# Two transformer layers on one core: the order of the small tasks between the attention scores, and where the last batches' feed-forward blocks stand

## The reference

```python
x = _layernorm(x + _L0_attn_ref(x, ...))   # 16 heads of 8, full softmax attention
x = _layernorm(x + _L0_ffn_ref(x, ...))    # 128 -> 512, butterfly, exact GELU, butterfly, 512 -> 128
x = _layernorm(x + _L1_attn_ref(x, ...))   # low-rank q and kv, rotary embedding (RoPE), causal attention
x = _layernorm(x + _L1_ffn_ref(x, ...))    # silu(x Wg^T) * (x Wu^T), then Wd^T; 384 hidden, int32 weights / 127
```

## Time and profile before

| | |
|---|---|
| median of 3 runs | 343.15 us (340.76 to 343.46) |
| the profiled execution | 346.31 us, of which the span of the trace is 344.2 us |
| PE busy | 308.4 us, 90% |
| DVE busy | 249.8 us, 73% |
| ACT, POOL busy | 184.2 us (54%), 178.3 us (52%) |
| mean granted clock of TensorE | 0.979 of full speed |

### The profile page before, as it was taken

One profiled execution on the slowest core, in us unless ns is written; L12 is line 12 of the kernel. 1 busy time (PEld: TensorE's weight loads), 2 busy tenths in 40 slices (PEclk: granted clock), 3 DMA queues, 4 the chain that ended last, 5 costly groups with the idle time before them and its releaser, 6 DMA issues.

```text
span 344.2 us, 10412 instructions
## 1 busy us (share of the span) xinstructions
PE 308.4 (90%) x3770; PEld 219.9 (64%) x3770; DVE 249.8 (73%) x941; ACT 184.2 (54%) x396; POOL 178.3 (52%) x299
## 2 busy tenths in 40 slices
PE   8799998899899998999899699899999999976862
PEld 4566665666486566766567457776777777755652
DVE  4897686769587785868839469697989898935454
ACT  3365675465946566565746337465556555545110
POOL 6595372210224252453627939397877747455621
PEclk9999999999999999999989789999999999999989
DMA  6733350011000110203011110111111200001000
GB/s 253 210 136 49 87 130 3 4 31 33 3 3 2 34 33 16 50 4 63 3 33 34 31 28 8 35 33 34 33 34 49 49 5 18 4 1 34 15 2 30
DMA packets 9470, 14.29 MB, mean 42 GB/s; under 512 B 2140, under 2 KB 5196, under 8 KB 9292
## 3 DMA queue, kind: packets, MB, share of 16 engines
q1 hardware_dynamic: 8988, 13.09, 15.3%
q10 hardware_dynamic: 432, 0.53, 0.4%
HBM read 6.28 MB, written 1.05 MB: 21 GB/s over the span
## 4 chain that ended last, share of the span: by engine, by line
PE 67%; DVE 13%; ACT 9%; issue 5%; POOL 2%; DMA 1%; POOLq 0%; SPq 0%; ACTq 0%; DVEq 0%
PE bank L379 19%; PE bank L571 13%; DVE mx L779 7%; PE bank L538 6%; PE bank L516 5%; PE bank L388 5%; PE bank L526 4%; PE bank L455 4%; PE bank L586 3%; ACT E L689 3%; PE bank L549 2%; PE bank L501 2%; DVE hid L803 2%; PE bank L440 1%; ACT L689 1%
## 5 line engine op out<-in xcount | busy, mean ns | idle before, releaser
L689 ACT ACTIVATE E<-bank 128x512 f32<-128x512 f32 (+1 forms) x256 | 120.4, 547 | 84.4 <-PE bank L388 83.2
L379 PE MATMUL bank<-QK 31*128 31x256 f32 (+1 forms) x1024 | 119.7, 369 | 10.6 <-DVE mx L779 4.0
L388 PE MATMUL bank<-QK 32*128 32x256 f32 (+1 forms) x1024 | 118.9, 372 | 0.0
L379 PEld LDWEIGHTS bank<-QK 31*128 31x128 f32 x1024 | 89.8, 186 | 34.7 <-issue 15.3
L779 DVE TENSOR_REDUCE mx<-bank 128x2 f32<-128x512 f32 x128 | 79.3, 684 | 19.1 <-PE bank L379 19.0
L388 PEld LDWEIGHTS bank<-QK 32*128 32x128 f32 x1024 | 86.7, 186 | 1.4 <-issue 0.4
L787 DVE CUSTOM_DVE_ANT_0 masked_s<-bank,mask_sb 128x256 f32<-128x256 f32 (+1 forms) x256 | 73.7, 353 | 12.4 <-PE bank L379 12.2
L571 PE MATMUL bank<-E,V 128*32 128x256 f32 (+1 forms) x1024 | 56.7, 363 | 3.9 <-ACT E L689 3.6
L969 POOL TENSOR_SCALAR_AFFINE_SELECT E<-E 128x512 f32<-128x512 f32 x64 | 39.0, 635 | 28.8 <-ACT E L689 28.7
L571 PEld LDWEIGHTS bank<-E,V 128*32 128x32 f32 x1024 | 29.9, 111 | 24.4 <-ACT E L689 4.8
L976 POOL TENSOR_TENSOR at<-turned,rec 128x256 f32<-128x256 f32 x16 | 10.1, 629 | 62.3 <-DVE rec L882 62.3
(11 more groups left out here) (107 smaller groups left out, 393.4 us busy)
## 6 DMA issues: line engine op xcount, KB each, us to landing
QK<-qk SPq DMA_DIRECT2D x60, 64.0 KB
rs<-ry SPq DMA_DIRECT2D x16, 128.0 KB, 2.3
xb<-x_nat SPq DMA_DIRECT2D x1, 1024.0 KB, 5.3
out<-ln_g SPq DMA_DIRECT2D x8, 128.0 KB, 1.9
xt<-x_t SPq DMA_DIRECT2D x1, 896.0 KB, 6.6
wi<-wi_all SPq DMA_DIRECT2D x1, 576.0 KB, 5.1
QK<-mt SPq DMA_DIRECT2D x32, 8.0 KB
fac<-fac_u SPq DMA_DIRECT2D x1, 508.0 KB, 6.0
```

Of the source, the lines that this page charges most:

```text
L379: ins = nc.tensor.matmul(g_bank["max", m][:, cols], q, QK[rows, b % QK_RING, r, 1, keys], start=True, stop=True)
L388: ins = nc.tensor.matmul(g_bank["exp", m][:, c * T:(c + 1) * T - q0], QK[rows, b % QK_RING, r, 1, c * P:(c + 1) * P], QK[rows, b % QK_RING ...
L689: act.activation(E[:, a % E_RING, j, 0:n], g_bank["exp", m][:, 0:n], ACT.Exp, scale=SCALE)\
```

## The change

It changes orders, banks and offsets; no operation on data is added but one: batch 15's last layer norm gets buffers of its own (`NL`), and batch 14's last normalisation moves from GpSimd to VectorE.

- **Banks** (`claim`): in layer 0 the extra tasks take `at`, `at+2`, `at+3`, `at+1` in this order, in layer 1 `at+2`, `at+3`, `at`, `at+1` as before, and in the step after a GELU `at`, `at+1`, ... as before. From step 240 on the exponentials always use banks 0 to 3 and the extra tasks banks 4 to 7.
- **TensorE and ScalarE**: the qk projection comes behind the turned maxima instead of last; up1 comes ahead of dn1. xt of the even batches 0, 2, 4 and 6 and of batch 14 stands one step later, xt of batch 15 one step earlier (`turned_at`). The constants JOIN and TURN (two small weight products) go from steps 20 and 32 to step 36.
- **VectorE**: in each step first what reads a bank (up0, gates, dn1's residual, proj's residual, `turned`, dn0's residual), then what does not (att, rec, all statistics). Four gates move to the end of later steps (`LATE_GATES`).
- **GpSimd**: the rotation stands behind the normalisations of its step.
- **The last FFNs**: new offsets for batches 12 to 15, which with batch 11's down projection share the last steps.

```diff
-FFN1.update({BATCHES - 4: ((40, 40, 48), 52, 56), BATCHES - 3: ((40, 40, 40), 44, 48),
-             BATCHES - 2: ((32, 36, 36), 44, 48), BATCHES - 1: ((36, 36, 36), 40, 44)})
-BXU, BXD, TURN, JOIN, BV, XB_AT, WF_AT, LATE = (0, 4), 16, 32, 20, 4, 16, 40, 0
+FFN1.update({BATCHES - 4: ((40, 40, 52), 60, 64), BATCHES - 3: ((40, 44, 52), 56, 64),
+             BATCHES - 2: ((36, 40, 44), 52, 56), BATCHES - 1: ((32, 32, 32), 40, 44)})
+LATE_GATES = {(BATCHES - 3, 2): HEADS + 4, (BATCHES - 2, 0): HEADS + 8, (BATCHES - 2, 1): HEADS + 12, (BATCHES - 2, 2): HEADS + 12}
+BXU, BXD, TURN, JOIN, BV, XB_AT, WF_AT, LATE = (0, 4), 16, 36, 36, 4, 16, 40, 0
+def turned_at(g):
+    for b in range(BATCHES):
+        late = b % 2 == 0 if b < NB else b < BATCHES - 1
+        if g == H * b + (AT_LN if b == BATCHES - 1 else AT_XT + QUAD if late else AT_XT):
+            return b
+    return None
...
                 assert i < QUAD
-                if NB * H <= g and tile_at(g - QUAD, AT_GELU) is None:
-                    i = (i + 2) % QUAD
+                if g + LEAD >= HEADS:
+                    return take(QUAD + i, task, semaphore, value)
+                if tile_at(g - QUAD, AT_GELU) is None:
+                    i = ((0, 2, 3, 1) if g < NB * H else (2, 3, 0, 1))[i]
                 return take(QUAD * (g // QUAD % 2) + i, task, semaphore, value)
...
-                    scores((), range(g, g + QUAD), at)
+                    scores((), range(g, g + QUAD), 0)
...
                     nc.vector.tensor_tensor((N1 if b < BATCHES - 1 else NL)["r"][:, :, :], ...)
-                    dve.wait_ge(F1["res_done"], i + 1)
-                    statistics(N1, 0, QT, F1["var_ready"])
...
-                    dve.wait_ge(A["res_done"], b + 1)
-                    statistics(NA, 0, QT, A["var_ready"])
                 if (n := products_at(g)) is not None:
...
+                if (b := ffn1_at(g, 1)) is not None:
+                    i = b - NB
+                    dve.wait_ge(F1["res_done"], i + 1)
+                    statistics(N1 if b < BATCHES - 1 else NL, 0, QT, F1["var_ready"])
+                    if b == BATCHES - 1:
+                        dve.wait_ge(last_ready, 2)
+                        dve.wait_ge(stored[(i - 1) % 2], 16 * ((i - 1) // 2))
+                        normalise_last(N1, (i - 1) % 2, F1["ln_ready"])
+                        dve.wait_ge(last_ready, 3)
+                        normalise_last(NL, 0, F1["ln_ready"])
+                if (b := attention_at(g, AT_PROJ)) is not None:
+                    dve.wait_ge(A["res_done"], b + 1)
+                    statistics(NA, 0, QT, A["var_ready"])
...
-                if (b := batch_at(g, AT_ROPE, (1,))) is not None:
...
-                    nc.gpsimd.tensor_tensor(qk[:, b % 2, :, :], ry[:, :, :], rs[:, :, :], ALU.add).then_inc(A["rotated"], 1)
...
                     normalise(N1, QT, i % 2, F1["ln_ready"])
+                if (b := batch_at(g, AT_ROPE, (1,))) is not None:
...
+                    nc.gpsimd.tensor_tensor(qk[:, b % 2, :, :], ry[:, :, :], rs[:, :, :], ALU.add).then_inc(A["rotated"], 1)
```

More of the change, by code:

```diff
@@ L517, in _ @@
                                          start=True, stop=True).then_inc(F0["up_ps"], 1)
+                for b, c in ups_at(g):
+                    i = b - NB
+                    bank = claim(("up1", i, c), F1["hid_ready"], SC * i + c + 1, g)
+                    if c == 0:
+                        pe.wait_ge(A["xt_ready"], b + 1)
+                        if i == 0:
+                            pe.wait_ge(wf_ready, 2)
+                    for s in range(2):
+                        ins = nc.tensor.matmul(bank[:, s * T:(s + 1) * T], wf[:, s, c * P:(c + 1) * P],
+                                               xt[:, i * T:(i + 1) * T], start=True, stop=True)
+                    ins.then_inc(F1["up_ps"], 1)
                 if (b := ffn1_at(g, 1)) is not None:
@@ L838, in _ @@
                             .then_inc(F0["pre_ready"], 1)
+                for b, c in ups_at(g):
+                    if (b, c) not in LATE_GATES:
+                        gate(b, c)
                 if (b := ffn1_at(g, 1)) is not None:
```

126 lines of the change are left out of this document (55 added, 71 removed).

## The result

The changed kernel takes 325.06 us (median of 4 runs, 324.64 to 325.32), the kernel before on the same chip 343.3 us (4 runs, 340.76 to 345.22). The ratio is 0.947, with an interval of 0.942 to 0.953. The forecast was 328 with a range of 320 to 336. The profiled execution took 324.64 us, its span is 322.8, where the one of before took 346.31 with a span of 344.2.

A forecast was written before the change was run, and what follows sets the result against it. TensorE's list of work was taken to set the time in the middle, a chain of waits the end. Gains 5.5 + 4.2 + 1.0 + 1.0 + 2.1 + 4.4 = 18.2 off the profiled 346.3 gave 328 us, range 320 to 336.

The forecast's parts named there:

- rotation: Step 140: with GpSimd's rotation behind the normalisation, TensorE's 2.97 us wait for `ln_a` and half clock go; 5.5 us.
- steps after a GELU: Steps 64, 96, 128: the product no longer waits for the first exponential; 4.2 us, 1.6 of it half clock.
- layer 0's banks, less the statistics: Layer 0: eight waits of 0.32 us for the second maximum go, less delays from later statistics; net 1.0 us.
- step 36: Step 36: JOIN, TURN and xt of batch 0 fill TensorE's 1.74 us wait for maxima; 1.0 us gained.
- layer 1: Layer 1, three batches: scores stop waiting for the third up projection's gate, with up1 first and statistics last; 2.1 us.
- end: From step 240 on: four 1.32 us waits for exponentials go; 6.8 us gained at full clock, net 4.4.
- VectorE late: Rival: statistics and att, moved behind a step's last wait, delay the maxima; 334 us, chance 0.16.
- Half clock to the end: Rival: from xt of batch 15 on, all 6.9 us run at 1.2 GHz; 332.5 us, chance 0.10.
- A new wait: Rival: causal cuts behind the rotation come late for step 148's product, and the clock falls; 333.5 us, chance 0.05.
- The slower case: Rival: each of 32 pairs of statistics lands on TensorE with its whole 0.75 us; 351 us, chance 0.04.
- nothing: Rival: half of what the slower rival charges, and no gain at the end; 342 us, chance 0.05.

The follow-up runs named there:

- the kernel with the filler: The changed kernel plus four matmuls of 512 columns, result unread, in TensorE's idle stretch behind batch 15's output projection; 323.85 us, ratio 0.939.
- the second trace of the changed kernel: The changed kernel run once more with no edit, as base for the other experiments; 326.63 us, ratio 0.949 to the kernel before.

## Why the prediction was right, step by step

| term | predicted | by the steps of the two traces | by its experiment |
|---|---|---|---|
| rotation | 5.5 | 4.3 | 4.2 undone (0.7 of it in step 112), 4.6 alone |
| steps after a GELU | 4.2 | 5.7 | 4.2 |
| layer 0's banks, less the statistics | 1.0 | 2.7 | banks 3.9, statistics 0.7 (both gains) |
| step 36 | 1.0 | 1.0 | none made |
| layer 1 | 2.1 | 2.1 | 2.2, and 0.9 at the end |
| end | 4.4 | 5.3 | banks 4.7, offsets 0.4 |
| start | 0 | 0.3 | scatter |
| sum | 18.2 | 21.4 | |

The bound was read rightly: what TensorE waits for and the half clock behind it were the gain. The waits for `ln_a`, behind the GELUs and for layer 1's gate went, those for exponentials at the end went from 5.3 to 0.95 us, that for a gate at the end from 2.17 to 0.93.

Taken one by one, the seven undone parts cost 4.2 + 0.7 + 3.9 + 4.2 + 4.7 + 0.4 + 3.1 = 21.2 us. That this is near 21.4 is chance. The 21.4 hold 0.3 of start, 1.0 of step 36 and 1.6 of half clock that no experiment undid; without them they are 18.5. So the parts do act on each other: undone one at a time, they cost 2.7 us more than they brought together, since a place left late costs more where all else is early. The 0.7 us in step 112 are such a case.

**The rotation** was 1.2 too large. "All 2.97 us go" failed: 0.97 of them turned into a wait for maxima at step 148. The clock's part was 2.4 us in the kernel before (the gain behind step 148), and 1.6 in the changed kernel with the rotation first, where I took 2.8. The wait for the causal cuts that I feared there did not come: they ended at 187.53 us and the product started at 188.04. (By the terms as written the product was to start at 201.0 less 5.5, which is 195.5 and not 196.4, ahead of the cuts.)

**The steps after a GELU**: the three waits went as forecast. I took 0.7 + 0.7 + 1.2 for them without the clock, the steps gained 1.3 + 1.3 + 1.5. The step that failed is the charge of 0.5 us for statistics that make the maxima late: with them early the steps are 0.13 us slower. The terms as written do not give the 0.7 either (1.14 less 0.37 less 0.5 is 0.27), so its nearness owes something to luck. The 1.6 us of half clock in the third were in the profiled execution, and not in that of the kernel with only the rotation moved. This is one reason why 21.7 us between the two profiled executions are 18.2 between the medians.

**Layer 0's banks and the statistics** is the term that was most wrong. I priced a place at 0.32 us, 2.6 in all, and took off 1 to 1.6 for statistics that come late in VectorE's list. The banks alone are worth 3.9, in thirteen places and not eight, and the statistics at the end of the step are a gain: 1.25 us up to step 240, of which 0.56 are given back at the end. I had counted VectorE's room ahead of the next maximum, 0.58 us for 0.8 us of work, and adding up durations was the error: instructions that follow one another overlap by some 0.1 us in the timeline, and in the step of the earlier trace rows it is 1.03 us from the start of `turned` to the next maximum (101.95 to 102.98) with the statistics between, against 1.02 without them before (106.01 to 107.03). They fit the room to 0.01 us. The gain itself is `turned` ahead of them in layer 1, and in layer 0 that they no longer stand right behind the residual they read.

**Step 36 and layer 1** came as forecast. No kernel took step 36 apart, so its 1.0 rests on the steps' times alone, and its cause is argued. Layer 1's 2.1 hold the statistics too (0.6 of their loss lies there), so up1 ahead of dn1 and they are not two separate gains.

**The end** was 0.9 too small, and its parts stand otherwise than the words "planned anew" suggest. Separate banks are 4.7 of it. The new offsets are 0.4, since of what they win ahead of step 252 (2.25) they lose 1.8 behind it, half clock included. The half clock itself, charged at 2.4, costs 1.7 against the kernel with the filler, and 0.8 more in the second trace of the changed kernel. From step 240 to the output projection the gain is 5.8 us, where I took 6 (and the terms written there give 5.7); from there to the last residual it is 12.5 us, that is 10.8 at full clock against the 11.3 of the forecast. So within rounding the 0.9 are 0.7 of half clock and 0.5 of chain, less 0.2. The idle stretch ahead of the last xt was forecast at 3.7 us and is 3.64; step 240 was forecast near 286 and stands at 283.6; 40 us were to follow it and 39.2 do.

**The sum.** Against the profiled execution the gain was 3.5 us larger than my sum (21.7 against 18.2). Layer 0 accounts for 1.7 of it, the GELU steps for 1.5, the end for 0.9, the start for 0.3, time outside the span for 0.3, and the rotation takes 1.2 off. The 325.06 us lie 3 below the forecast for that reason. That the 18.2 agree with the difference of the medians (343.3 to 325.06) is luck and no merit of the sum: the profiled execution of before lay 3 us above its median. Four of its other executions had a mean clock of 0.999 and took 340.6 to 341.1 us, so they had next to no half clock, behind the wait of 2.97 us neither. The 2.4 us of the rotation's clock are thus no gain against each execution.

**The rivals.** VectorE late is refuted by the time and, for the statistics, by the kernel that has them early; att and rec at the end of the step and the earlier qk projection had no run of their own. Half clock to the end did not come: the last two down projections (314.64) take 2.84 us together, the 2.8 of the forecast, and as long in the kernel with the filler. A new wait came, but for maxima and at 0.97 us, not for the cuts. The slower case would have needed a full 0.75 us for each pair of statistics; the largest loss seen for a pair is 0.2, and it is a loss of the early place. The rival "nothing" was mis-added: half of 23 us and the 4.4 of the end on top of 328 give 344, not 342.

## What to carry to other kernels

Where engines work through written lists and share banks, order each list by who waits for the bank that an instruction frees: what reads a bank first, what only computes last, and let a task take the bank whose reader is done first (3.9 us in layer 0, 4.7 at the end, 4.2 behind the GELUs). Price a removed wait against the next one in line (here 0.97 of 2.97 us came back as another), do not add up the parts undone one by one as if they stood alone (21.2 against 18.5 us), and set the sum against the profiled execution only after asking which of its losses the other executions share. New offsets are worth an experiment of their own: here they were 0.4 of 5.3 us.

## What the runs showed of the hardware

The start of the program scatters by more than most parts of the change are worth: step 20 begins between 39.4 and 42.9 us in the traces, in the changed kernel later by 2.4 us where the clock is 0.72 from 18 to 24 us than where it is 1.00. The clock is not all of it: with layer 0's old banks the clock is 1.00 there and step 20 begins at 41.40 us. From step 32 to step 240, over 230 us, the two traces of the changed kernel agree to 0.03 us.

The granted clock behind an idle wait is not the same in each execution. Behind the same 1.31 us it was 0.70 once and 1.00 once. Behind 2.17 and 2.18 us the next down projection ran at about half clock (2.74 and 2.90 us instead of 1.57), behind 2.25 us the clock stayed at 1.00. Behind 3.64 to 3.78 us at the end it fell in each of eight traces, to 0.68 to 0.80 over the next 8.2 us; with 3.6 us of unused matmuls in the gap it stayed at 1.00.

An instruction of VectorE that reads the result of the one just before it starts later than one that does not: 0.46 against 0.35 us behind the start of a residual of 0.42 us.
